# Expert and shared products in three float32r terms, tokens scattered to expert rows in DRAM, and two of four shared groups ahead of the experts

## What is computed

```python
# attention: corr = ifft(fft(q) * conj(fft(k))).real, its 8 largest lags, softmax over them,
# out = sum over the 8 lags of w_i * v shifted by lag_i (clamped at the end)
x = x + autocorrelation(layernorm(x), ctx, ctx)
x2 = layernorm(x).reshape(-1, 512)
g_s, u_s = split(x2 @ shared_w_gate_up.T)
shared_out = silu(g_s) * u_s @ shared_w_down.T
probs = softmax(x2 @ gate_w.T)
topk_vals, topk_idx = top_k(probs, 2); topk_vals /= topk_vals.sum()
gu = einsum('th,eih->eti', x2, w_gate_up); g, u = split(gu)
out_e = einsum('eti,ehi->eth', silu(g) * u, w_down)
x = x + (einsum('eth,te->th', out_e, combine) + shared_out)
```

## Time and profile before

| | before |
|---|---|
| median of 3 runs | 511.94 us (511.39 to 512.33) |
| span of the profiled execution | 511.9 us |
| PE busy | 478.7 us (94%), 2097 instructions |
| DVE busy | 312.0 us (61%) |
| ACT busy | 222.6 us (43%) |
| POOL busy | 228.1 us (45%) |
| DMA | 66.66 MB, mean 130 GB/s |
| chain that ended last | PE 59%, DVE 16%, issue 10%, POOL 8%, ACT 4%, DMA 2% |

### The profile page before, as it was taken

How to read it: one execution, slowest core, us unless ns; L and a number is a source line. 1 busy time by engine, 2 the same in 40 slices (tenths; PEclk the granted TensorE clock), 3 DMA queues, 4 the chain that set the end, 5 groups by cost and what they waited for, 6 DMA issues and landing times.

```text
span 511.9 us, 8881 instructions
## 1 busy us (share of the span) xinstructions
PE 478.7 (94%) x2097; PEld 328.7 (64%) x2098; DVE 312.0 (61%) x972; ACT 222.6 (43%) x425; POOL 228.1 (45%) x384
## 2 busy tenths in 40 slices
PE   3699999999999999898999999999999999999997
PEld 1556655666566555455577767666776678888885
DVE  2779999899999864794223333333333466747643
ACT  4768887887888854400022222222222345122120
POOL 2355666767666744035333333333333026466520
PEclk9889999999999999999899999999999999999999
DMA  4416434324142220801335455555545323465622
GB/s 153 165 41 227 145 95 172 108 98 143 61 143 83 102 104 20 345 5 41 100 117 160 149 158 158 164 164 155 149 152 158 124 97 111 141 186 165 207 61 82
DMA packets 24914, 66.66 MB, mean 130 GB/s; under 512 B 3456, under 2 KB 3456, under 8 KB 23488
## 3 DMA queue, kind: packets, MB, share of 16 engines
q1 hardware_dynamic: 18576, 45.74, 24.7%
q0 software_dynamic: 6320, 20.71, 15.5%
HBM read 45.73 MB, written 20.71 MB: 130 GB/s over the span
## 4 chain that ended last, share of the span: by engine, by line
PE 59%; DVE 16%; issue 10%; POOL 8%; ACT 4%; DMA 2%; DVEq 0%; POOLq 0%; SPq 0%; ACTq 0%
PE bank L469 19%; PE bank L667 17%; PE bank L682 8%; PE bank L655 4%; DVE stats L898 3%; PE bank L570 2%; DVE top_v L935 2%; PE bank L579 2%; POOL arena L1210 2%; PE bank L481 2%; POOL arena L1213 2%; DVE resid L923 2%; DVE arena L944 1%; DVE arena L940 1%; DVE arena L909 1%
## 5 line engine op out<-in xcount | busy, mean ns | idle before, releaser
L667 PE MATMUL bank<-wgu_sb,x2T 128*128 x376 | 91.9, 388 | 2.3 <-issue 0.7
L667 PEld LDWEIGHTS bank<-wgu_sb,x2T 128*128 128x128 f32 x376 | 67.6, 189 | 40.9 <-issue 33.6
L826 ACT COPY x2T<-bank 128x512 f32<-128x512 f32 x47 | 27.5, 586 | 143.2 <-PE bank L655 143.2
L1263 POOL DMA_INDIRECT xg_sb<-x_rows,gidx x47 | 45.9, 976 | 98.4 <-PE bank L655 93.9
L1095 DVE COPY actT_both<-bank 128x128 f32<-128x128 f32 x47 | 13.7, 292 | 73.2 <-PE bank L676 73.2
L469 PE MATMUL bank<-act_lo 128*128 128x512 f32 x96 | 41.0, 536 | 8.4 <-DVE act_lo L977 8.4
L682 PE MATMUL bank<-arena,actT_both 128*128 x94 | 47.9, 593 | 0.0
L469 PE MATMUL bank<-tokens_hi,shgu_hi 128*128 128x512 f32 x92 | 36.2, 394 | 0.0
L469 PE MATMUL bank<-tokens_hi,shgu_lo 128*128 128x512 f32 x92 | 35.8, 389 | 0.0
L469 PE MATMUL bank<-tokens_lo,shgu_hi 128*128 128x512 f32 x92 | 35.8, 389 | 0.0
L469 PEld LDWEIGHTS bank<-act_lo 128*128 128x128 f32 x96 | 18.6, 196 | 24.7 <-issue 23.3
(11 more groups left out here) (153 smaller groups left out, 1083.1 us busy)
## 6 DMA issues: line engine op xcount, KB each, us to landing
y_rows<-x2T SPq DMA_DIRECT2D x47, 256.0 KB, 3.1
wgu_sb<-w_gu SPq DMA_DIRECT2D x8, 1024.0 KB, 5.2
resid<-x SPq DMA_DIRECT2D x16, 256.0 KB, 2.8
arena<-ctx SPq DMA_DIRECT2D x16, 256.0 KB, 4.0
x_rows<-arena SPq DMA_DIRECT2D x16, 256.0 KB, 2.1
result<-resid SPq DMA_DIRECT2D x16, 256.0 KB, 2.2
arena<-w_down SPq DMA_DIRECT2D x1, 3072.0 KB, 12.7
shgu_sb<-sh_gu SPq DMA_DIRECT2D x1, 2048.0 KB, 8.9
```

What stands on the lines that cost most here:

```text
L667: last = mm(ps_gu[b][:, 0:2 * INTER], xgT[b][:, c * P:(c + 1) * P], wgu_sb[:, bass.ds(at + c * 2 * INTER, 2 * INTER)], start=c == 0, stop= ...
L826: copy(xgT[b], ps_xgT[:, :]).then_inc(xgT_ready, 1)
L1263: nc.gpsimd.indirect_dma_start(xg[b], None, x2_rows[:, :], bass.IndirectOffsetOnAxis(ap=gidx[b][:, 0:1], axis=0)).then_inc(gathered[b], 16)
```

## The change

1. **Experts in three float32r terms.** Gate, up and down products go through `split_product`; token halves come from PSUM (high half ACT, low half DVE), also the activation's halves. The expert weights no longer lie whole in SBUF: an expert's gate, up and down weights (`EXPERT` = 1536 columns) are loaded one at a time, split by POOL into high and low halves, and kept in a ring of 3 experts (`RING`). POOL refills a slot when the tiles of the expert that held it are done.
2. **Where a tile's weights lie** is packed with the number of weight splits to wait for in one word (`tile_word`); PE still reads two words per tile, both at the start of a tile's turn, and takes them apart with register arithmetic. The router's weight is applied when the results are added (`add_results`), not in the experts.
3. **Tokens scattered.** The one-hot products are gone. The normalised tokens are loaded back from `x2_rows` into 4 bounce buffers by SP, and POOL scatters each tile twice (once per choice) to `xs_rows` in DRAM with an indirect DMA by `pos_i`: 32 scatters. SP then loads an expert tile with a plain DMA. `xs_rows` is filled with zeros during attention (11 DMAs, 12 MB).
4. **All four shared groups split; groups 0 and 1 ahead of the experts**, groups 2 and 3 behind. The shared weights (`shw`, 12 chunks of 512 columns) are split during attention, one chunk per iteration from 2 to 13, at the end of ACT's and of POOL's iteration; the tokens of group 0 are split at the end of iteration 14. PE's fillers in the last iterations are the same products, now split.
5. No copies of indices ahead of the indirect DMAs.

Cut to its core:

```diff
+            def gate_up(h, b, word):
+                j = 2 * h + b
+                at = weights_at(word)
+                pe.wait_ge(w_ready, word % WORD)
+                pe.wait_ge(xgT_ready, j + 1)
+                for c in range(KB):
+                    last = split_product(ps_gu[b][:, 0:2 * INTER],
+                                         of_halves(xgT_halves[b], lambda x: x[:, c * P:(c + 1) * P]),
+                                         of_halves((w_hi, w_lo), lambda w: w[:, bass.ds(at + c * 2 * INTER, 2 * INTER)]),
+                                         c == 0, c == KB - 1)
+                last.then_inc(gu_psum, 1)
             def expert(h, b, n):
...
+                if n is None or n + 1 < SLOT_TILES:
+                    coming = tile_word_of(j + 1)
+                if n is None or n >= 2:
+                    leaving = tile_word_of(j - 2)
+                if n is None or n + 2 < SLOT_TILES:
+                    transposes(h + 1, b)
...
                 if n is None or n >= 2:
-                    mm(ps_y[b][:, :], actT_sb[b], wd_sb[:, bass.ds(at, D)], start=True, stop=True).then_inc(down_psum, 1)
+                    split_product(ps_y[b][:, :], actT_halves[b],
+                                  of_halves((w_hi, w_lo), lambda w: w[:, bass.ds(at + KB * 2 * INTER, D)]),
+                                  True, True).then_inc(tiles_done, 1)
+                if n is None or n + 1 < SLOT_TILES:
+                    gate_up(h + (b + 1) // 2, (b + 1) % 2, coming)
```

```diff
 ACT, end of an attention iteration
+                if n is None or 2 <= n < 2 + SHW // D:
+                    chunk = 2 * h + b - 2
+                    act.wait_ge(shw_loaded, 16)
+                    copy(tile_of(shw_hi, chunk), tile_of(shw_in, chunk)).then_inc(shw_hi_ready, 1)
+                if n == PAIRS - 2:
+                    for t in range(GT):
+                        tokens_hi_split(0, t)
 POOL, behind attention
-            for s in range(HOT_TURNS):
...
+            split_weights(0)
+            for t in range(GT):
+                tokens_lo_split(1, t)
+            split_weights(1)
+            pool.wait_ge(pos_ready, 1)
+            pool.wait_ge(xs_zeroed, 16 * (PAIRS - 5))
+            for t in range(PAIRS):
+                buf, turn = t % BOUNCES, t // BOUNCES
+                pool.wait_ge(bounced[buf], 16 * (turn + 1))
+                for k in range(CHOICES):
+                    col = k * PAIRS + t
+                    nc.gpsimd.indirect_dma_start(xs_rows[:, :], bass.IndirectOffsetOnAxis(ap=pos_i[:, col:col + 1], axis=0),
+                                                 bounce[buf], None).then_inc(scattered[buf], 16)
+            split_weights(2)
 SP
+            for buf in range(BOUNCES):
+                sp.wait_ge(scattered[buf], 16 * CHOICES * PAIRS // BOUNCES)
+            sp.wait_ge(tile_word_ready, 1)
+            for j in range(6):
+                load_xg(j // 2, j % 2)
 PE, ahead of the experts
-            slots(range(0, 2))
...
+            shared_down(0)
+            for m in range(SB):
+                for part in range(2):
+                    shared_half(1, m, part)
+            shared_down(1)
```

More of the change, by code:

```diff
@@ L723, in _ @@
+            pe.wait_ge(y_ready, SLOT_TILES)
+            shared_down(2)
+            for m in range(SB):
+                for part in range(2):
+                    shared_half(3, m, part)
+            shared_down(3)
         @block.scalar
@@ L836, in _ @@
-            act.wait_ge(sh_up_psum, SB)
-            gathered_T(0, 0)
-            for n in range(2):
-                expert(0, n, n)
-            with act.Fori(1, SLOT_TILES // 2) as h:
+                if n is None or n < SLOT_TILES:
+                    act.wait_ge(gu_psum, j + 1)
+                    wait(act, act_ready, j)
+                    nc.scalar.activation(silu_sb[:, 0:INTER], ps_gu[b][:, 0:INTER], ACT.Silu).then_inc(silu_ready, 1)
+                if n is None or n + 2 < SLOT_TILES:
+                    gathered_hi(h + 1, b)
@@ L841, in _ @@
+            act.wait_ge(sh_up_psum, 2 * SB)
+            for j in range(2):
+                gathered_hi(0, j)
+            act.wait_ge(sh_out_psum, 2 * GT)
+            for n in range(4):
+                expert(n // 2, n % 2, n)
+            with act.Fori(2, SLOT_TILES // 2 - 1) as h:
                 for b in range(2):
                     expert(h, b, None)
-            expert(SLOT_TILES // 2, 0, SLOT_TILES - 1)
-            def weights_hi(first, last):
-                for part, m in WEIGHT_BLOCKS[first:last]:
-                    copy(weight_block(shgu_hi, part, m), weight_block(shgu_sb, part, m)).then_inc(weights_hi_ready, 1)
@@ new lines, in expert @@
+                if n is None or n + 2 < SLOT_TILES:
+                    gathered_lo(h + 1, b)
+                if n is None or 1 <= n <= SLOT_TILES:
+                    dve.wait_ge(actT_hi_ready, j)
+                    hi, lo = actT_halves[1 - b]
+                    tt(lo, ps_actT[:, 0:P], hi.bitcast(F32), ALU.subtract).then_inc(actT_ready, 1)
+            for j in range(2):
+                gathered_lo(0, j)
+            for n in range(4):
+                expert(n // 2, n % 2, n)
+            with dve.Fori(2, SLOT_TILES // 2 - 1) as h:
@@ L1108, in _ @@
                 for b in range(2):
                     expert(h, b, None)
-            expert(SLOT_TILES // 2, 0, SLOT_TILES - 1)
+            for n in range(SLOT_TILES - 3, SLOT_TILES):
+                expert(n // 2, n % 2, n)
             def add_results(quad, u):
@@ L1267, in _, with load_weights @@
+            def load_weights(e):
+                buf, loaded, _ = weights_turn(e)
+                nc.gpsimd.dma_start(weight_in[buf], w_exp[:, e * EXPERT:(e + 1) * EXPERT]).then_inc(loaded, 16)
+            pool.wait_ge(out_psum, PAIRS)
+            pool.wait_ge(x2T_psum, PAIRS)
+            pool.wait_ge(sh_act_ready, 1)
             for b in range(2):
                 pool.wait_ge(x2_stored[b], 16 * PAIRS // 2)
-                gather(0, b)
-            with pool.Fori(1, SLOT_TILES // 2) as h:
-                for b in range(2):
-                    gather(h, b)
```

599 lines of the change are left out of this document (271 added, 328 removed).

## The result

The changed kernel takes 550.48 us (median of 4 runs, 549.46 to 551.7). The kernel before took 511.66 us on the same chip. The ratio is 1.076, 95% interval 1.0736 to 1.0784. The profiled execution of the changed kernel has a span of 547.8 us. The forecast was 523 with a range of 494 to 546: right in direction, too low by 25 us against the span (547.8 - 523), and outside its range.

What follows compares the result with a forecast made beforehand. PE was busy throughout and its instruction queue nearly full, so the queue was to pace the experts. First gate product 284.6, 161 us of tiles to 447, group 2 from 452, groups 2 and 3 to 519, tail about 4.5: 523, range 494 to 546.

Steps and rivals of the forecast that it cites:

- Attention, 211.7: Last logits at 211.7 us: 206.7 plus 5, mainly 12 iterations losing 0.4 us each to ACT's added cast.
- the low end: Scatters on POOL: 0.97 us each, 31 us for 32, the 0.81 us ahead of each being hidden.
- rival 2: Scatters on POOL take 1.78 us each, 57 us instead of 35, total 545; chance 0.15.
- The bounce round: Token reload through 4 bounce buffers: 7.7 us per round against 4 x 1.95 of scatters, just even.
- The first tile: Start of the experts: 1.8 us for transposes, high and low half, from tile loaded (282.8) to first gate product (284.6).
- Experts, 3.5 per tile: Expert loop: PE's instruction queue sets 7.1 us per turn of two tiles, 161 us for 46 tiles.
- the base of 6.0 us: Expert loop: work of PE's queue per turn before the change, taken from 5.8 to 6.2 us.
- Behind the experts, 4.8 us: After the last gate product: group 2's tokens are split while PE has one down product, 4.8 us, until 452.
- 1, the queue does not bind: Expert loop: table loads overlap queued products, the array sets 2.7 us per tile, 37 us less, 486; chance 0.17.
- 3, each matmul costs the queue 0.06 us: Expert loop: 18 more matmuls per tile cost PE's queue 1.1 us, 51 us in all, total 574; chance 0.02.
- 4, the lead chain is hidden: Ahead of the experts: ACT's idle time takes the casts, scatters start at the positions' time, total 508 to 514; chance 0.12.
- 5, POOL's splits starve the experts: Expert loop: weight splits over 9 us on POOL hold up experts, each further us costing 13; chance 0.01.

Runs made afterwards that it cites:

- the fillers: Changed kernel with one table load per tile, scatters ahead of splits, cast behind logits, plus 46 useless products in PE's two idle stretches: 502.0 us, ratio 0.9809.
- the constant address: Changed kernel without table reads in PE's expert tiles; every product takes its weights from the ring's first slot: 515.9 us, ratio 1.0084.
- the kernel with scatters ahead: Changed kernel with POOL's scatters ahead of its splits of group 1's tokens (moved to DVE) and expert 1's weights: 548.4 us, repeated 539.2 us.

## Why the prediction was wrong, step by step

**Attention, 211.7: the size held, the cause only in part.** Measured 212.6, inside the bounds; the same attention code gave 212.2 to 215.0 in other traces, so the 0.9 says little. "0.4 us are lost per iteration", put down to the place of the cast, failed: another place gives back 0.09 per iteration. "POOL's subtraction fits: it idles 0.82 and 1.07 us around it" failed too: alone it makes an iteration 0.3 us longer, and cast and subtraction together 0.58. That the sum came out is luck. The idle times of the earlier trace rows are waits for other engines, which in turn wait for POOL (ACT, PE, DVE, POOL and back). That work put behind them delays POOL's next step instead of filling them is a reading of these runs; the ring itself was not tested.

**Groups 0 and 1, 271.5: right**, PE was free at 272.8.

**Scatters: the low end was taken, and it failed.** "I take the low end" rested on one row, the copy at 420.78 that starts as the gather ends. From start to start it is 1.265 us: 0.96 and 0.30. The low end had 0.97 and the high end 1.78, so rival 2 was no truer. The bounce round, 7.7 us with two scatters in it, was too low as well: with one scatter it would be 6.7, and 8.4 was measured. POOL's own 10.1 us hid that. Of the 8.8 us that the last scatter was late, 7 are from here.

**The first tile: 1.8 us forecast, 3.9 measured.** The 1.8 had the transposes and halves of one tile. The kernel transposes two tiles before the first gate product, and the second waits for DVE to read the first. With half of the scatters, where PE has no gap and its clock stays at 1.00, that way still takes 3.4 us (274.2 to 277.6), and 3.6 with the fillers. So 0.3 to 0.5 us is the clock and the rest this order of work.

**The clock** "will fall", the text said, "and come back in the first tile or two", which it did, but it got no price, and its fall behind the second idle stretch was not foreseen. There it cost 2.4 us, which the fillers gave back.

**Experts, 3.5 per tile: right in mechanism, mis-sized.** The queue sets the pace, as the forecast said, against its main rival. Its sum, 6.0 + 1.1 = 7.1 us per turn, was 0.55 short. The term that failed is the base of 6.0 us, not the price of an address: ten second addresses were put at 0.11 each and cost 0.115, so the base in the changed kernel is 7.65 - 1.15 = 6.5. In it stands the long table load, 0.33 us more than another. The earlier trace rows has a load of 311 ns, of `tile_down_at`, and all loads were priced by it; those of `tile_gu_at` have a median of 676 ns in the same loop. How much of the 6.0 was such a load, and what the rest of the 0.5 is, no run took apart. The bounds 3.3 to 3.7 were too narrow for a sum of over 50 small prices.

**Behind the experts, 4.8 us: right** (467.7 to 472.5). Then 12 products at half the clock, and a tail of 5.5 instead of 4.5 us.

**Rivals.** 1, the queue does not bind: refuted by one load per tile (38 us off the stage, with all products kept). Its figure for the array, 2.7 us per tile, is what the constant address gave. 3, each matmul costs the queue 0.06 us: refuted, by 6.17 against 6.14 to 6.29. 4, the lead chain is hidden: PE idled 17.7 us. 5, POOL's splits starve the experts: in the changed kernel POOL waits 72 us in all for PE to free a slot of the ring, so not that.

**The range** ended at 546. It joined the cases as if they excluded each other. But dearer scatters, a longer way to the first product, a dearer queue and a lower clock came together.

## What to carry to other kernels

Before halving an engine's work, count what its instruction queue does per unit of that work: table loads, addresses, semaphore waits. If that sum is near the time now, less work in the array gains nothing, and the first edit is in the queue (a word kept in a register, operands that share an address). Idle time next to an instruction is room for more work only if nobody waits for what comes behind it. And where a stage is put behind a chain of DMAs, start the chain at its first true dependence, ahead of work that merely stood there first.

## What was not expected of the hardware

In eight traces PE slows down in group 1, while the scatters run. Here the run of one load per tile, repeated, timeline of PE:

```profile
284.50 0.39 PE L452 MATMUL bank<-shw_hi,act_lo 128*128 128x512 f32 x1
284.73 0.39 PE L452 MATMUL bank<-shw_hi,act_hi 128*128 128x512 f32 x1
285.97 0.39 PE L452 MATMUL bank<-shw_lo,act_hi 128*128 128x512 f32 x1 [0.86 <-issue]
287.37 0.40 PE L452 MATMUL bank<-shw_hi,act_lo 128*128 128x512 f32 x1 [1.01 <-issue]
288.08 0.50 PE L452 MATMUL bank<-shw_hi,act_hi 128*128 128x512 f32 x1 [0.31 <-issue]
```

Products stand 0.23, then up to 2.1 us apart, the profile shows no semaphore that they wait for, and none starts for 11.5 us from 266.9 on (24.8 us in the run with the constant address). This trace has as many products as that of the changed kernel, 2320, so none are missing from it. In all eight it begins 21.7 to 22.4 us behind the first scatter (243.3 and 265.3, 240.2 and 262.2, for two). PE reaches the first expert tile 7.5 to 16.0 us behind the start of the last scatter, against 5.4 to 5.7 in the traces without it, so it costs 2 to 10 us. It does not belong to a kernel: the kernel with scatters ahead had it in one run and not in the other. Of kernels run together, one after the other on a chip, either all their traces had it or none. The traces with it hold 5304 to 5456 semaphore events, those without 6244 or 6246 (5989 with half of the scatters), so part of what happened is not recorded.

The Trainium skill, page "NOTIFIC — the notification-queue block", section "7.1 Overflow: three behaviours, one of which stalls the engine", names three things that the path which writes such records can do when a ring is full: drop the new record, overwrite the oldest, or hold back the engine; a queue is set to one of them. Missing events would be one of the first two and slow products the third, and no run here tells which of them happened, or whether both follow from the DMA traffic. All times of this study carry a profile, so the cause stays open.

Also not expected: once per turn a table load that follows another in the same tile takes long, 587 ns in the turn shown, where the rest took 301 to 304, and this ends when ten register instructions or two loads of the turn go. And a float32r product of 256 columns keeps its 0.12 us beside a DMA share of 0.57.
